# First layer of a recurrent network: a second add of the query products on POOL, key squares on ACT, and a later preparation

## The chip, the cores and the metric

The kernel runs on one core of a Trainium2 chip. The metric is the time of the whole program on the device in microseconds (us), as the median of several runs. The engines named below are PE (the matrix engine), DVE (VectorE), ACT (ScalarE), POOL (GpSimd) and SP, which issues transfers. They run side by side and are held together by counting semaphores.

## What is computed

The network has four layers; each takes a layer norm of `x`, computes a recurrent part `s` and a gate `g`, and sets `x = x + s * g`. The change touches the first layer alone, whose recurrent part is a gated delta rule with 16 heads of size 8 over 256 steps of 32 sequences:

```python
q = (x @ Wq + bq); k = (x @ Wk + bk); v = (x @ Wv + bv)      # each reshaped to heads of D = 8
k = k / (norm(k, axis=-1) + 1e-06)
beta = sigmoid(x @ Wbeta + bbeta)
def step(S, q_t, k_t, v_t, beta_t):
    Sk = einsum('bhde,bhe->bhd', S, k_t)
    S = S + beta_t * einsum('bhd,bhe->bhde', v_t - Sk, k_t)
    return S, einsum('bhde,bhe->bhd', S, q_t)                # output of the step
```

Its output goes through `Wo`, and is gated by the silu of a feed forward part (relu, square, two ternary weight matrices).

## The kernel before

`delta_ffn` runs the first layer. The tokens are cut into NT = 16 tiles of 512 tokens, which are 16 time steps of 32 sequences; one tile is worked off as 8 pairs of steps (PAIRS = 8). The state of the recurrence goes from pair to pair, so the pairs form one long chain of 128, all of it on DVE (`pair`, L569 to L597: two instructions each of the lines L576, L581, L584, L587, L594 and L597). The other engines prepare the next tile and finish the last one beside this chain. Each engine's order is written out by hand in its own block; the engines wait for each other only by semaphores, and an engine never passes a waiting instruction.

What one tile i needs, and what is done for tile i + 1 while the pairs of tile i run:

- ACT evacuates the projections of tile i + 2 from PSUM (`evacuate`, L393, four per tile, the fourth with a sigmoid, which needs a table load) once DVE has turned the tile before (semaphore `turned`). Then comes the square root of the key norms (`root`, L398, with a table load of its own), then the feed forward work.
- DVE turns the four projections of tile i + 1 to token-major form (`turn`, L543), sums the squares of the keys (`norms`, L547), adds 1e-6 and inverts after ACT's root (`inverse`, L551 and L553), and sums the overlap of the two keys of a pair (`overlaps`, L557).
- POOL squares the keys (`squares`, L454), multiplies values by beta (`values`, L460), scales the keys (`keys`, L466 and L470) and multiplies them with each other (L473, what `overlaps` sums), and corrects for the second step of a pair (`correct`, L482 and L485). DVE begins a tile when `prepared` and `lifted` (an ACT copy of the corrected keys to PSUM, L422) are there.
- The outputs: after each pair POOL multiplies the state with the queries (`queries`, L493, 512 products per partition). After every second pair POOL adds the upper half of each group of eight products to the lower half (`halve`, L499), and DVE sums the remaining four (`outputs`, L561). The last quarter of a tile's outputs is summed in the next tile, followed by the turn back (`turn_out`, L568). PE projects it, and POOL gates it (`gate`, L504 and L507, after the multiplication of pair 6 of the next tile).

The names in profile rows carry the prefix `d_`: `d_sq_q` holds the products with the queries, `d_tm` the turned projections, `d_nrm` the norms, `d_sqk` the squared keys.

Of the kernel before, what the change touches and what calls it, by code (L numbers as in the profile page):

```python
# [7 lines left out]
ALU = mybir.AluOpType  # L8
ACT = mybir.ActivationFunctionType
AX = mybir.AxisListType.X  # L10

P = 128
# [3 lines left out]
NT = N // TILE  # L16
# [4 lines left out]
@contextmanager  # L21
def phase(nc, names, inside=None):

    stage = nc.next_id()
    sems = [nc.alloc_semaphore(f"{n}_{stage}") for n in names.split()]
    if inside is not None:
        block, held = inside
        held.extend(sems)
        yield (block, *sems)
        return  # L30
    with nc.Block() as block:
        yield (block, *sems)
    nc.clear_and_free_semaphores(sems)
    nc.all_engine_barrier()  # L34
# [222 lines left out]
H0, D0 = 16, 8  # L257
# [5 lines left out]
def delta_ffn(nc, w, wfc_t, wproj_t, xn, x_in, x_out, x_slots):  # L263
# [7 lines left out]
    with ExitStack() as ctx:  # L271
        def sb(name, shape):
            return ctx.enter_context(nc.sbuf_tensor("d_" + name, shape, F32))
# [8 lines left out]
        tm = sb("tm", [P, 2, 4, TILE])  # L282
        sqk = sb("sqk", [P, STEPS * HL, D0])
# [9 lines left out]
        sq_q = sb("sq_q", [P, STEPS, HL * D0, D0])  # L293
        o_tm = sb("o_tm", [P, TILE])
# [6 lines left out]
        zeros = sb("zeros", [P, TILE])  # L301
        (block, projected, evacuated, turned, sqk_ready, norm2, norm1, shifted, rn_ready, parts, m_ready, c_ready, prepared, s_gated,
         stepped, state_ready, sq_ready, o_part, o_turned, o_projected, s_ready, h_ready, relu_ready, r2_ready, y_ready,
         g_ready, mixed, lifted, gated, zeroed, cleared, halved, x_in0, x_in1) = ctx.enter_context(phase(
             nc, "projected evacuated turned sqk_ready norm2 norm1 shifted rn_ready parts m_ready c_ready prepared s_gated "
             "stepped state_ready sq_ready o_part o_turned o_projected s_ready h_ready relu_ready r2_ready y_ready "
             "g_ready mixed lifted gated zeroed cleared halved x_in0 x_in1"))
        x_ready = (x_in0, x_in1)
        rows_out = x_slots.rearrange("(i p r q) c -> i p r (q c)", p=P, r=4, q=4)
        CLEARS = x_slots.shape[0] // (16 * P)  # L310
# [2 lines left out]
        def slot(a, n):  # L313
            return (max(0, a - 3) + n) % 2

        def out_slot(a):
            return a % 2

        def up_slot(a, n):
            return (a + n) % 2  # L320
# [63 lines left out]
        @block.scalar  # L384
        def _(act):

            def evacuate(a):

                if a:
                    act.wait_ge(turned, a)  # L390
                for n, name in enumerate(("bq", "bk", "bv", "bbeta")):
                    act.wait_ge(projected, a * 4 + n + 1)
                    nc.scalar.activation(fm[:, n], ring[:, slot(a, n)], ACT.Identity if n < 3 else ACT.Sigmoid,  # L393
                                         bias=w[name]).then_inc(evacuated, 1)

            def root(a):
                act.wait_ge(norm2, a + 1)
                nc.scalar.activation(nrm[:], nrm[:], ACT.Sqrt).then_inc(norm1, 1)  # L398

            def out(a):  # L400
                act.wait_ge(o_projected, a + 1)
                if a >= 2:
                    act.wait_ge(gated, a - 1)
                nc.scalar.activation(s[:, a % 2], ring[:, out_slot(a)], ACT.Identity, bias=w["bo"]).then_inc(s_ready, 1)

            def ffn(a):
                for m in range(M):
                    n = a * M + m
                    act.wait_ge(h_ready, n + 1)
                    nc.scalar.activation(r[:, m % 2], ring[:, up_slot(a, m)], ACT.Relu).then_inc(relu_ready, 1)  # L410
                    act.wait_ge(relu_ready, n + 1)
                    if a:
                        act.wait_ge(y_ready, n - M + 1)
                    nc.scalar.activation(r2[:, m], r[:, m % 2], ACT.Square).then_inc(r2_ready, 1)
                act.wait_ge(y_ready, (a + 1) * M)
                if a >= 2:
                    act.wait_ge(gated, a - 1)
                nc.scalar.activation(g[:, a % 2], down[:], ACT.Silu).then_inc(g_ready, 1)

            def lift(a):  # L420
                act.wait_ge(prepared, a * 2 + 1)
                nc.scalar.activation(kb_up[:, a % 2], kb[:, a % 2], ACT.Copy).then_inc(lifted, 1)  # L422

            evacuate(0)
            root(0)
            evacuate(1)
            lift(0)
            for i in range(NT):
                if i + 2 < NT:
                    evacuate(i + 2)  # L430
                if i + 1 < NT:
                    root(i + 1)
                if i:
                    out(i - 1)
                ffn(i)
                if i + 1 < NT:
                    lift(i + 1)
            out(NT - 1)

        @block.gpsimd  # L440
        def _(pool):
            G = nc.gpsimd

            def by_step(ap, f):
                return ap.rearrange("p (t h d) -> p t (h d)", h=HL, d=D0)[:, :, f * HH * D0:(f + 1) * HH * D0]
# [2 lines left out]
                b = tm[:, a % 2, 3].rearrange("p (t c) -> p t c", c=HD)[:, :, f * HH:(f + 1) * HH]  # L448
                return b.unsqueeze(3).broadcast_to([P, STEPS, HH, D0])

            def squares(a):
                pool.wait_ge(turned, a + 1)
                kk = tm[:, a % 2, 1].rearrange("p (th d) -> p th d", d=D0)
                G.tensor_tensor(sqk[:], kk, kk, ALU.mult).then_inc(sqk_ready, 1)  # L454

            def values(a):
                if not a:
                    pool.wait_ge(turned, 1)
                for f in range(2):
                    G.tensor_tensor(vb[:, a % 2, :, f], by_step(tm[:, a % 2, 2], f), beta(a, f), ALU.mult).then_inc(parts, 1)  # L460

# [34 lines left out]
            def halve(i, j):  # L496
                pool.wait_ge(sq_ready, i * PAIRS + 2 * j + 2)
                both = sq_q[:, 4 * j:4 * j + 4].rearrange("p t h e -> p (t h) e")
                G.tensor_tensor(both[:, :, 0:D0 // 2], both[:, :, 0:D0 // 2], both[:, :, D0 // 2:], ALU.add).then_inc(halved, 1)  # L499

            def gate(a):
                pool.wait_ge(s_ready, a + 1)
# [6 lines left out]
                                xt[:, a % 2].rearrange("p (t b) -> p t b", b=B), ALU.add).then_inc(gated, 1)  # L509

            G.memset(zeros[:], 0.0).then_inc(zeroed, 1)
            squares(0)
            values(0)
            keys(0)
            correct(0)
            for i in range(NT):
                more = i + 1 < NT
                for p in range(PAIRS):
                    queries(i, p)
                    if p % 2:  # L520
                        halve(i, p // 2)
                    if p == 0 and more:
                        squares(i + 1)
                    if p == 1 and more:
                        values(i + 1)
                    if p == 3 and more:
                        keys(i + 1)
                    if p == 5 and more:
                        correct(i + 1)
                    if p == 6 and i:  # L530
                        gate(i - 1)
# [3 lines left out]
        def _(dve):  # L535
            V = nc.vector

            def turn(a):

                dve.wait_ge(evacuated, a * 4 + 4)  # L540
                if a >= 2:
                    dve.wait_ge(sq_ready, (a - 1) * PAIRS)
                V.transpose(tm[:, a % 2].rearrange("p n c -> p (n c)"), fm[:].rearrange("p n c -> p (n c)")).then_inc(turned, 1)  # L543

            def norms(a):
                dve.wait_ge(sqk_ready, a + 1)
                V.tensor_reduce(nrm[:], sqk[:], AX, ALU.add).then_inc(norm2, 1)  # L547
# [9 lines left out]
                V.tensor_reduce(c[:], cross[:], AX, ALU.add).then_inc(c_ready, 1)  # L557

            def outputs(i, j):
                dve.wait_ge(halved, i * 4 + j + 1)  # L560
                V.tensor_reduce(o_tm[:, j * P:(j + 1) * P], sq_q[:, 4 * j:4 * j + 4].rearrange("p t h e -> p (t h) e")[:, :, 0:D0 // 2],  # L561
                                AX, ALU.add).then_inc(o_part, 1)

            def turn_out(i):
# [39 lines left out]
            for i in range(NT):  # L604
                more = i + 1 < NT
                dve.wait_ge(lifted, i + 1)
                dve.wait_ge(prepared, 2 * i + 2)
                for p in range(PAIRS):
                    pair(i, p)
                    if p == 0 and more:  # L610
                        turn(i + 1)
                    if p == 1 and i:
                        outputs(i - 1, 3)
                        turn_out(i - 1)
                    if p == 1 and more:
                        norms(i + 1)
                    if p == 2 and more:
                        inverse(i + 1)
                    if p in (3, 5, 7):
                        outputs(i, p // 2 - 1)  # L620
                    if p == 5 and more:
                        overlaps(i + 1)
            outputs(NT - 1, 3)
            turn_out(NT - 1)

# [2800 lines left out]
```

## Time and profile before

| what | value |
|---|---|
| median of 3 runs | 4978.35 us (4972.01 to 4992.69) |
| the profiled execution | 4953.71 us, its span 4952.1 us |
| busy in the span: PE, DVE | 3799.2 us (77%), 3628.7 us (73%) |
| busy in the span: POOL, ACT | 2954.5 us (60%), 2514.5 us (51%) |
| first pair of the first layer starts, last state is done | 76.7 us, 569.9 us |
| of this stretch, one tile in steady state | 31.20 us |

A row of the timeline gives the start of an instruction, its length, the engine, the line and what it writes and reads; `x2` is two of them in a row, and the bracket at the end is the time in which the engine was idle before, and who released it. On DVE an instruction starts before the one ahead of it has drained, so the distance between two starts is some hundredths of a microsecond shorter than the duration of the first. This distance is called the slot of an instruction here.

### The profile page before, as it was taken

Reading aid. Unit: us, or ns where it says so; the run is one execution under the profiler, and the core shown is the slowest. Engines: PE = TensorE matmul, PEld = TensorE weight load, DVE = VectorE, ACT = ScalarE, POOL = GpSimd, SP = SyncE. Lnnn points to the kernel's source line nnn. Section 1 sums busy time; section 2 is a strip of 40 time slices with the busy share of each in tenths; the row PEclk is TensorE's granted clock in tenths of the full one; section 3 lists DMA queues with packets and bytes.
Section 4 is the critical chain, followed back from the end, with each engine's and each line's share of the span. In section 5 each row is a group of like instructions: output and inputs, shape, how many; then the busy total and the mean of one; then the engine's idle time right before and its main releaser. Section 6 shows DMA issues by size and latency. Waiting matters only on the chain. (4 is left out here: it accounts for less than half of the span.)

```text
span 4952.1 us, 46565 instructions
## 1 busy us (share of the span) xinstructions
PE 3799.2 (77%) x13159; PEld 1741.4 (35%) x13222; DVE 3628.7 (73%) x5288; ACT 2514.5 (51%) x3881; POOL 2954.5 (60%) x2245
## 2 busy tenths in 40 slices
PE   5444475999649978888887799898979777777776
PEld 2111122764216633333332455453423222222222
DVE  6999774124547669999998644555543899999998
ACT  4444431344437766666664344445355655555554
POOL 3888566017254469999994311114420899889987
PEclk7777788999869999999999899999989999999998
DMA  1110201213211134444441423221200444444343
GB/s 50 43 43 9 84 34 52 68 55 82 94 54 58 43 129 155 156 155 154 155 156 69 97 41 45 41 38 48 64 7 34 144 135 139 136 136 141 128 141 98
DMA packets 161698, 434.77 MB, mean 88 GB/s; under 512 B 28150, under 2 KB 51384, under 8 KB 160048
## 3 DMA queue, kind: packets, MB, share of 16 engines
q1 hardware_dynamic: 142512, 374.41, 25.0%
q0 software_dynamic: 18944, 57.57, 3.4%
q8 instruction: 98, 1.61, 0.1%
q14 instruction: 144, 1.18, 0.1%
HBM read 363.67 MB, written 68.68 MB: 87 GB/s over the span
## 5 line engine op out<-in xcount | busy, mean ns | idle before, releaser
L1659 ACT ACTIVATE mb_h<-m_dt,m_a_neg 128x512 f32<-128x512 f32 x1024 | 665.0, 681 | 724.0 <-DVE r L1814 333.6
L1518 PE MATMUL mb_y<-r,m_diag_y 128*128 128x512 f32 x1024 | 548.5, 671 | 273.2 <-POOL r L1739 164.6
L1805 DVE TENSOR_TENSOR_SCAN mb_h<-mb_h,m_u 128x1024 f32<-128x1024 f32 x320 | 734.0, 2294 | 10.8 <-DVE mb_h L1794 0.5
L1762 POOL TENSOR_TENSOR m_u<-m_bsb,m_xs 128x1024 f32<-128x1024 f32 x256 | 600.1, 2368 | 175.6 <-DMA m_bsb<-bc_rows 175.6
L1762 POOL TENSOR_TENSOR m_u<-m_bsb,m_dtx 128x1024 f32<-128x1024 f32 x256 | 596.1, 2360 | 49.7 <-DVE m_dtx L1846 27.9
L1518 PE MATMUL mb_y<-m_hc,w_common 128*128 128x512 f32 x1024 | 497.0, 625 | 151.8 <-DVE m_hc L1814 85.7
L1805 DVE TENSOR_TENSOR_SCAN m_hs<-mb_h,m_u 128x1024 f32<-128x1024 f32 x192 | 437.6, 2279 | 1.7 <-POOL m_u L1762 1.7
L1518 PEld LDWEIGHTS mb_y<-r,m_diag_y 128*128 128x128 f32 x1024 | 196.2, 207 | 620.0 <-POOL r L1739 244.9
L2288 DVE TENSOR_REDUCE at_mx<-at_ps_s 128x4 f32<-128x512 f32 (+1 forms) x256 | 242.8, 957 | 218.7 <-PE at_ps_s L2102 218.6
L1739 POOL TENSOR_TENSOR r<-m_hs,m_csb 128x1024 f32<-128x1024 f32 x128 | 308.3, 2409 | 117.1 <-DVE m_hs L1805 116.7
L1518 PEld LDWEIGHTS mb_y<-m_hc,w_common 128*128 128x128 f32 x1024 | 191.1, 197 | 450.0 <-issue 192.0
L2220 ACT ACTIVATE at_pt<-at_ps_c 128x512 f32<-128x512 f32 x384 | 229.4, 608 | 160.8 <-DMA r<-y_slots,l_slots 60.8
L2246 POOL CAST at_nm<-at_mx 128x16 bf16<-128x16 f32 x64 | 12.6, 196 | 500.1 <-DVE at_mx L2288 500.1
L1791 DVE SCALAR_TENSOR_TENSOR m_u<-mb_h,m_u 128x1024 f32<-128x1024 f32 x256 | 307.8, 1202 | 0.0
L343 PE MATMUL d_ring<-r,w_l 128*128 128x512 f32 x128 | 91.2, 856 | 224.1 <-ACT d_fm L393 222.2
L1477 PE MATMUL mb_w<-r,m_wconv 128*128 128x512 f32 x512 | 233.2, 609 | 14.1 <-PEq L34 7.0
L1814 DVE TENSOR_TENSOR m_hc<-mb_h,m_csb 128x1024 f32<-128x1024 f32 x192 | 235.1, 1224 | 3.6
L493 POOL TENSOR_TENSOR d_sq_q<-d_state,d_tm 128x512 f32<-128x512 f32 x128 | 161.7, 1269 | 91.2 <-DVE d_state L597 91.1
L1009 POOL DMA_INDIRECT x_slots<-r,l_slots x128 | 142.9, 1117 | 86.8 <-DVEq L1053 45.3
L2127 PE MATMUL at_ps_c<-at_q,at_k 75*128 75x512 bf16 x384 | 154.1, 402 | 43.5 <-ACT at_pt L2220 27.7
L1739 POOL TENSOR_TENSOR m_hc<-m_hs,m_csb 128x1024 f32<-128x1024 f32 x64 | 150.8, 2356 | 32.4 <-DVE m_hs L1805 32.4
L2102 PE MATMUL at_ps_s<-at_k,at_q 72*128 72x256 bf16 (+1 forms) x1024 | 169.6, 260 | 0.0
(516 smaller groups left out, 8475.4 us busy)
## 6 DMA issues: line engine op xcount, KB each, us to landing
m_bsb<-bc_rows SPq DMA_DIRECT2D x256, 512.0 KB, 4.9
m_csb<-bc_rows SPq DMA_DIRECT2D x256, 512.0 KB, 4.0
at_q<-q_parts SPq DMA_DIRECT2D x144, 128.0 KB
x_slots<-d_zeros SPq DMA_DIRECT2D x8, 1024.0 KB, 5.1
kept_x<-r SPq DMA_DIRECT2D x2, 4096.0 KB, 14.1
xg_xg<-x_slots SPq DMA_DIRECT2D x32, 256.0 KB, 2.7
y_slots<-xg_yo POOLq DMA_DIRECT2D x32, 256.0 KB, 2.3
xl_xg<-x_slots SPq DMA_DIRECT2D x32, 256.0 KB, 2.7
```

The lines of the kernel that those rows point to most:

```text
L493: G.tensor_tensor(sq_q[:, 2 * p:2 * p + 2], state[:, n % 3], qt.unsqueeze(2).broadcast_to([P, 2 * HL, D0, D0]), ALU.mult).then_inc(sq_read ...
L1477: mm = nc.tensor.matmul(ps_w[:, h], wconv[:, k, h * P:(h + 1) * P], padded_tile(hp, k)(a), start=k == 0, stop=k == TAPS - 1)
L1518: mm = nc.tensor.matmul(ps_y[:, h], weight, hc[:, q % RING, s], start=False, stop=g == GROUPS - 1 and s == SG - 1)
L1659: ins = nc.scalar.activation(ps_h[:, q % 2, s], dt[:, i % 2, h], ACT.Exp, scale=a_neg[:, n:n + 1])
L1739: nc.gpsimd.tensor_tensor(hc[:, q % RING], hs[:, k % 2], csb[:, n % RING], ALU.mult).then_inc(hp_ready, 1)
L1762: nc.gpsimd.tensor_tensor(u[:, q % RING], bsb[:, n % RING], dtx[:, i % 2, h].unsqueeze(1).broadcast_to([P, SG, TILE]), ALU.mult).then_inc( ...
L1791: V.scalar_tensor_tensor(out=flat(u[:, q % RING]), in0=flat(ps_h[:, q % 2]), scalar=-1.0, in1=flat(u[:, q % RING]), op0=ALU.add, op1=ALU.m ...
L1805: V.tensor_tensor_scan(flat(to), flat(ps_h[:, q % 2]), flat(u[:, q % RING]), 0.0, ALU.mult, ALU.add).then_inc(h_ready, 1)
L1814: V.tensor_tensor(hc[:, q % RING], ps_h[:, q % 2], csb[:, n % RING], ALU.mult).then_inc(hc_ready, 1)
L2102: mm = nc.tensor.matmul(ps_s[:, g % 2, d, 0:keys], q9[0:PARTS, slot, g * QPK + d, col:col + P], k9[0:PARTS, slot, g, row:row + keys], star ...
L2220: nc.scalar.activation(pt[:, u % 8], ps_c[:, u % 2], ACT.Exp).then_inc(exp_ready, 1)
L2288: V.tensor_reduce(mx[:, n % 2, g * QPK:(g + 1) * QPK], ps_s[:, g % 2, :, 0:(n % 2 + 1) * P], AX, ALU.max, negate=True).then_inc(max_ready, 1)
```

## The change

Three things are edited, all in `delta_ffn`.

- `halve` on POOL gets a second add: it waits for its own first add, then adds the products 2 and 3 of each group to 0 and 1 (new semaphore `summed`). `outputs` on DVE waits for `summed` and sums two values per output instead of four.
- The squares of the keys move from POOL to ACT (`squares`, new on ACT). ACT runs them for tile i + 1 ahead of `evacuate(i + 2)`.
- The preparation of tile i + 1 comes one pair later on DVE: `turn` after pair 1 instead of pair 0 (behind the last outputs and the turn back of the tile before), `norms` after pair 2 instead of 1, `inverse` after pair 3 instead of 2. On POOL `values` comes at pair 2 instead of 1, `keys` at pair 4 instead of 3. `correct` on POOL and `overlaps` on DVE stay at pair 5.

```diff
+            def squares(a):
+                act.wait_ge(turned, a + 1)
+                nc.scalar.activation(sqk[:].rearrange("p th d -> p (th d)"), tm[:, a % 2, 1], ACT.Square).then_inc(sqk_ready, 1)
...
             evacuate(0)
+            squares(0)
             root(0)
             evacuate(1)
             lift(0)
             for i in range(NT):
+                if i + 1 < NT:
+                    squares(i + 1)
                 if i + 2 < NT:
                     evacuate(i + 2)
...
                 G.tensor_tensor(both[:, :, 0:D0 // 2], both[:, :, 0:D0 // 2], both[:, :, D0 // 2:], ALU.add).then_inc(halved, 1)
+                pool.wait_ge(halved, i * 4 + j + 1)
+                G.tensor_tensor(both[:, :, 0:2], both[:, :, 0:2], both[:, :, 2:4], ALU.add).then_inc(summed, 1)
...
-                    if p == 0 and more:
-                        squares(i + 1)
-                    if p == 1 and more:
+                    if p == 2 and more:
                         values(i + 1)
-                    if p == 3 and more:
+                    if p == 4 and more:
                         keys(i + 1)
                     if p == 5 and more:
                         correct(i + 1)
...
             def outputs(i, j):
-                dve.wait_ge(halved, i * 4 + j + 1)
-                V.tensor_reduce(o_tm[:, j * P:(j + 1) * P], sq_q[:, 4 * j:4 * j + 4].rearrange("p t h e -> p (t h) e")[:, :, 0:D0 // 2],
+                dve.wait_ge(summed, i * 4 + j + 1)
+                V.tensor_reduce(o_tm[:, j * P:(j + 1) * P], sq_q[:, 4 * j:4 * j + 4].rearrange("p t h e -> p (t h) e")[:, :, 0:2],
                                 AX, ALU.add).then_inc(o_part, 1)
...
                     pair(i, p)
-                    if p == 0 and more:
-                        turn(i + 1)
                     if p == 1 and i:
                         outputs(i - 1, 3)
                         turn_out(i - 1)
                     if p == 1 and more:
+                        turn(i + 1)
+                    if p == 2 and more:
                         norms(i + 1)
-                    if p == 2 and more:
+                    if p == 3 and more:
                         inverse(i + 1)
                     if p in (3, 5, 7):
                         outputs(i, p // 2 - 1)
                     if p == 5 and more:
                         overlaps(i + 1)
```

On DVE, in the middle of the first layer, this stands from the turn of the next tile (L543) to the sum of its squared keys (L547) before:

```order
L543 STREAM_TRANSPOSE d_tm<-d_fm 128x2048
L576 TENSOR_TENSOR d_prod<-d_state,d_kb_up 128x256 x2
L581 TENSOR_REDUCE d_small<-d_prod 128x32 x2
L584 TENSOR_TENSOR d_small<-d_vb,d_small 128x32 x2
L587 TENSOR_TENSOR d_outer<-d_small,d_k 128x256 x2
L594 TENSOR_TENSOR d_state<-d_state,d_outer 128x128 x2
L597 TENSOR_TENSOR d_state<-d_state,d_outer 128x128 x2
L561 TENSOR_REDUCE d_o_tm<-d_sq_q 128x128
L568 STREAM_TRANSPOSE d_o_fm<-d_o_tm 128x512
L547 TENSOR_REDUCE d_nrm<-d_sqk 128x64
```

and now, with the outputs of the tile before ahead of it:

```order
L561 TENSOR_REDUCE d_o_tm<-d_sq_q 128x128
L568 STREAM_TRANSPOSE d_o_fm<-d_o_tm 128x512
L543 STREAM_TRANSPOSE d_tm<-d_fm 128x2048
L576 TENSOR_TENSOR d_prod<-d_state,d_kb_up 128x256 x2
L581 TENSOR_REDUCE d_small<-d_prod 128x32 x2
L584 TENSOR_TENSOR d_small<-d_vb,d_small 128x32 x2
L587 TENSOR_TENSOR d_outer<-d_small,d_k 128x256 x2
L594 TENSOR_TENSOR d_state<-d_state,d_outer 128x128 x2
L597 TENSOR_TENSOR d_state<-d_state,d_outer 128x128 x2
L547 TENSOR_REDUCE d_nrm<-d_sqk 128x64
```

The last quarter of the outputs and the turn back have moved ahead of the turn, so that fewer instructions lie between the turn and what follows from it.

On ACT, at the same place, this stands from the copy of the corrected keys to the root of the norms before:

```order
L422 ACTIVATE d_kb_up<-d_kb 128x512
L393 ACTIVATE d_fm<-d_ring,w_l_63 128x512 x3
L393 ACT_TABLE_LOAD
L393 ACTIVATE d_fm<-d_ring,w_l_63 128x512
L398 ACT_TABLE_LOAD
L398 ACTIVATE d_nrm<-d_nrm 128x64
```

and now (the numbers of lines behind the new function have moved by 4):

```order
L426 ACTIVATE d_kb_up<-d_kb 128x512
L398 ACTIVATE d_sqk<-d_tm 128x512
L393 ACTIVATE d_fm<-d_ring,w_l_63 128x512 x3
L393 ACT_TABLE_LOAD
L393 ACTIVATE d_fm<-d_ring,w_l_63 128x512
L402 ACT_TABLE_LOAD
L402 ACTIVATE d_nrm<-d_nrm 128x64
```

The square stands ahead of the four evacuations and the root, and brings no table load of its own.

On POOL, this stands around the scaling of the keys (L466 to L473), from the products of pairs 2 and 3 on, before:

```order
L493 TENSOR_TENSOR d_sq_q<-d_state,d_tm 128x512 x2
L499 TENSOR_TENSOR d_sq_q<-d_sq_q 128x128x4
L466 TENSOR_TENSOR d_k<-d_tm,d_nrm 128x8x32 x2
L470 TENSOR_TENSOR d_kb<-d_k,d_tm 128x8x32 x2
L473 TENSOR_TENSOR d_cross<-d_k,d_kb 128x256
```

and now, from the products of pair 3 on:

```order
L494 TENSOR_TENSOR d_sq_q<-d_state,d_tm 128x512
L500 TENSOR_TENSOR d_sq_q<-d_sq_q 128x128x4
L502 TENSOR_TENSOR d_sq_q<-d_sq_q 128x128x2
L494 TENSOR_TENSOR d_sq_q<-d_state,d_tm 128x512
L467 TENSOR_TENSOR d_k<-d_tm,d_nrm 128x8x32 x2
L471 TENSOR_TENSOR d_kb<-d_k,d_tm 128x8x32 x2
L474 TENSOR_TENSOR d_cross<-d_k,d_kb 128x256
```

The keys now stand behind the products of pair 4, which wait for the state of that pair, and a second add stands behind each first one.

## Rows read from the trace of the kernel before

**Rows 1.** One steady tile: window; busy PE, PEld, DVE, ACT, POOL; clock; DMA share; GB/s

```profile
297.05:328.25 31.20, 13.97 (x26) 5.31 (x26) 30.85 (x106) 13.20 (x19) 25.39 (x27) 0.72 0.12 42
```

**Rows 2.** Timeline of DVE in this tile

```profile
297.05 2.31 DVE L543 STREAM_TRANSPOSE d_tm<-d_fm 128x2048 f32<-128x2048 f32 x1 [0.26 <-POOL d_sq_q L493]
299.28 0.71 DVE L576 TENSOR_TENSOR d_prod<-d_state,d_kb_up 128x256 f32<-128x256 f32 x2
...
303.60 0.64 DVE L547 TENSOR_REDUCE d_nrm<-d_sqk 128x64 f32<-128x512 f32 x1
304.16 0.74 DVE L576 TENSOR_TENSOR d_prod<-d_state,d_kb_up 128x256 f32<-128x256 f32 x2
...
307.15 0.19 DVE L551 TENSOR_SCALAR d_nrm<-d_nrm 128x64 f32<-128x64 f32 x1
...
307.85 0.69 DVE L576 TENSOR_TENSOR d_prod<-d_state,d_kb_up 128x256 f32<-128x256 f32 x2
...
317.38 0.68 DVE L561 TENSOR_REDUCE d_o_tm<-d_sq_q 128x128 f32<-128x512 f32 x1
317.97 0.41 DVE L557 TENSOR_REDUCE d_c<-d_cross 128x32 f32<-128x256 f32 x1
318.30 0.74 DVE L576 TENSOR_TENSOR d_prod<-d_state,d_kb_up 128x256 f32<-128x256 f32 x2
```

**Rows 3.** Lines of DVE and POOL in the first layer (count | busy us, mean ns | idle before)

```profile
L561 DVE TENSOR_REDUCE d_o_tm<-d_sq_q 128x128 f32<-128x512 f32 x64 | 43.3, 677 | 2.9 <-POOL d_sq_q L499 2.9
L543 DVE STREAM_TRANSPOSE d_tm<-d_fm 128x2048 f32<-128x2048 f32 x15 | 34.7, 2310 | 3.9 <-POOL d_sq_q L493 3.9
L454 POOL TENSOR_TENSOR d_sqk<-d_tm 128x512 f32<-128x512 f32 x16 | 16.6, 1039 | 12.3 <-DVE d_tm L543 12.3
```

**Rows 4.** Timeline of ACT in this tile, from the end of the turn on

```profile
299.39 1.26 ACT L393 ACTIVATE d_fm<-d_ring,w_l 128x512 f32<-128x512 f32 x2 [7.51 <-DVE d_tm L543]
...
304.95 1.28 ACT L398 ACT_TABLE_LOAD   x1
306.25 0.26 ACT L398 ACTIVATE d_nrm<-d_nrm 128x64 f32<-128x64 f32 x1
...
308.92 0.63 ACT L414 ACTIVATE d_r<-d_r 128x512 f32<-128x512 f32 x1
309.46 0.58 ACT L410 ACTIVATE d_r<-d_ring 128x512 f32<-128x512 f32 x1
```

**Rows 5.** Timeline of all engines in tile 0, from which two engines stand

```profile
79.69 2.30 DVE L543 STREAM_TRANSPOSE d_tm<-d_fm 128x2048 f32<-128x2048 f32 x1
...
88.36 0.26 ACT L398 ACTIVATE d_nrm<-d_nrm 128x64 f32<-128x64 f32 x1
...
88.65 0.26 DVE L551 TENSOR_SCALAR d_nrm<-d_nrm 128x64 f32<-128x64 f32 x1
...
89.42 0.69 DVE L576 TENSOR_TENSOR d_prod<-d_state,d_kb_up 128x256 f32<-128x256 f32 x2
```

**Rows 6.** Timeline of POOL in the steady tile

```profile
307.31 1.28 POOL L493 TENSOR_TENSOR d_sq_q<-d_state,d_tm 128x512 f32<-128x512 f32 x1 [1.08 <-DVE d_state L597]
310.95 1.28 POOL L493 TENSOR_TENSOR d_sq_q<-d_state,d_tm 128x512 f32<-128x512 f32 x1 [2.35 <-DVE d_state L597]
312.31 1.27 POOL L499 TENSOR_TENSOR d_sq_q<-d_sq_q 128x512 f32<-128x512 f32 x1
313.54 1.25 POOL L466 TENSOR_TENSOR d_k<-d_tm,d_nrm 128x256 f32<-128x256 f32 x2
...
316.06 0.73 POOL L473 TENSOR_TENSOR d_cross<-d_k,d_kb 128x256 f32<-128x256 f32 x1
...
320.54 0.63 POOL L482 TENSOR_TENSOR d_corr<-d_kb,d_c 128x256 f32<-128x256 f32 x1
...
323.09 1.26 POOL L493 TENSOR_TENSOR d_sq_q<-d_state,d_tm 128x512 f32<-128x512 f32 x1
...
326.88 1.26 POOL L493 TENSOR_TENSOR d_sq_q<-d_state,d_tm 128x512 f32<-128x512 f32 x1
```

More of the change, by code:

```diff
@@ L303, in delta_ffn @@
          stepped, state_ready, sq_ready, o_part, o_turned, o_projected, s_ready, h_ready, relu_ready, r2_ready, y_ready,
-         g_ready, mixed, lifted, gated, zeroed, cleared, halved, x_in0, x_in1) = ctx.enter_context(phase(
+         g_ready, mixed, lifted, gated, zeroed, cleared, halved, summed, x_in0, x_in1) = ctx.enter_context(phase(
              nc, "projected evacuated turned sqk_ready norm2 norm1 shifted rn_ready parts m_ready c_ready prepared s_gated "
              "stepped state_ready sq_ready o_part o_turned o_projected s_ready h_ready relu_ready r2_ready y_ready "
-             "g_ready mixed lifted gated zeroed cleared halved x_in0 x_in1"))
+             "g_ready mixed lifted gated zeroed cleared halved summed x_in0 x_in1"))
         x_ready = (x_in0, x_in1)
@@ L449, in beta, with values @@
                 return b.unsqueeze(3).broadcast_to([P, STEPS, HH, D0])
-            def squares(a):
+            def values(a):
                 pool.wait_ge(turned, a + 1)
[L453 to L458, printed above, removed]
                 for f in range(2):
@@ L511, in _ @@
             G.memset(zeros[:], 0.0).then_inc(zeroed, 1)
-            squares(0)
             values(0)
```

## The prediction, written before the changed kernel had run

> **What bounds the kernel now.** I read the busy time by engine first, then, since the change touches the first layer alone, one steady tile of it, and then the timelines of DVE, ACT and POOL in that tile. In the 31.20 us of a tile DVE is busy for 30.85 us, POOL for 25.39 us and ACT for 13.20 us [rows 1]. DVE's order is fixed, and its only wait is one ahead of the turn, for POOL's last product: 3.9 us in all, in 13 tiles [rows 3]. So DVE sets the pace here; whatever takes time off its slots shortens the layer, and every wait put into its row lengthens it. POOL and ACT have room in busy time, but DVE also waits for single results of theirs, and when these come is the question.
>
> **What DVE saves.** Summing 512 products into 128 outputs takes 677 ns [rows 3] and a slot of 0.59 us (317.38 to 317.97) [rows 2]. The new form reads 256. The nearest row is the reduction of 256 into 32, 0.41 us with a slot of 0.33 us [rows 2]; that of 512 into 64 takes 0.64 us against 0.68 us for 512 into 128 [rows 2], so the greater number of outputs adds some 0.03 us. I take a slot of 0.36 us, with ends 0.33 and 0.40. That is 64 x 0.23 = **14.7 us** less (12.2 to 16.6). The wait ahead of the turn goes too: the turn now stands behind pair 1, long after the last product of the tile before. With the overlap of neighbours that a wait breaks, it costs some 0.36 us per tile, 13 x 0.36 = **4.7 us** less. Together -19.4 us.
>
> **The wait at `inverse`.** This comes from the order on DVE and ACT. Before, ACT begins at 299.39, as soon as the turn is over (297.05 + 2.31 = 299.36), and its four evacuations, two table loads and the root end at 306.25 + 0.26 = 306.51 [rows 2, 4]. So the root is there 7.15 us behind the end of the turn. DVE comes for it at 307.15, 7.79 us behind the turn: 0.64 us of slack. Now both change for the worse. On ACT the square stands ahead of the evacuations; a square of this size has a slot of 0.54 us (308.92 to 309.46) [rows 4], I take 0.57, which makes the root 7.72 us late, 7.75 us with the handover of 0.03 (88.36 + 0.26 = 88.62 to 88.65) [rows 5]. The evacuation of the values waits for a product on PE that itself waits for the first evacuation, so the whole chain shifts. On DVE, outputs and turn back no longer lie in between: the way is turn (slot 299.28 - 297.05 = 2.23), pair 2 (2.97), `norms` (304.16 - 303.60 = 0.56), pair 3 (307.15 - 304.16 = 2.99) [rows 2], 8.75 us from the start of the turn, 6.44 us from its end. DVE waits 7.75 - 6.44 = **1.31 us**. That such a wait exists is shown by tile 0 of the kernel before, which has no outputs in between: there L551 starts at 88.65, 0.03 us behind the end of the root [rows 5]. A woken DVE also needs 0.77 us for the two instructions (88.65 to 89.42) instead of 0.70 [rows 2, 5], so 1.38 us. Tiles 1 to 13 have it, 13 x 1.38 = 17.9 us; tile 0 has no table load for the sigmoid, its root comes 6.63 us (88.62 - 81.99) behind the turn [rows 5] and would come at 7.23: some 0.6 us more than before. Tile 14 evacuates nothing. Sum **+18.5 us**.
>
> **The wait at `overlaps`.** `keys` moved behind pair 4, `overlaps` stayed behind pair 5. Call D the moment at which DVE has issued pair 4. POOL takes up the product 0.16 us later (307.15 to 307.31) [rows 2, 6]. Its slot is 1.23, the keys take 316.06 - 313.54 = 2.52, and the cross product 0.73 [rows 6]; with a handover of 0.05 the overlap can start at D + 0.16 + 1.23 + 2.52 + 0.73 + 0.05 = D + 4.69. DVE comes to it after pair 5 (3.00) and one sum of outputs (0.36), at D + 3.36. It waits **1.33 us**. Before, the keys stood behind pair 3 and had a whole pair more. 15 tiles, **+19.9 us**. I see nothing that covers this: POOL is idle ahead of pair 4's product, so it cannot be earlier than the state.
>
> **The second add on POOL.** 64 adds of 128 x 256. The rows of that size take 0.64 us (L466, two in 1.25) to 0.73 us (L473) [rows 6]; both operands are whole here as in L473, so 0.73, slot 0.69. Each also waits for the first add: a dependent start costs 1.36 instead of 1.23 (310.95 to 312.31) [rows 6], 0.13 more. Per tile 4 x 0.82 = 3.3 us, less one square of 1.04 us [rows 3]: POOL goes from 25.4 to some 27.6 us, under DVE's. Its order matters in one place, the last quarter. From D: product 5 at 4.59, first add 5.95, second 7.31, `correct` 8.00 (2.55 long, 320.54 to 323.09), product 6 at 10.55, gate and all until product 7 at 14.34 (3.79 later, 323.09 to 326.88), first add 15.70, second 17.06 to 17.79 [rows 6]. DVE, from D: overlap 4.69, two pairs 11.02, outputs 11.38, two pairs of the next tile 17.35, and then it wants the last quarter. That was covered before, since it had no second add; now it waits some 0.45 us. With 0.64 us per add it would be 0.25. I take 0.4, in the 14 tiles that have a gate before them: **+5.6 us**. The keys for the next tile are ready at 10.55, DVE wants them at 11.38, and ACT's copy fits in between, so the tile's start is covered. At the very end one more add and one shorter sum stand in line: +0.6 us.
>
> A rule of the Trainium skill bears on this price alone. "GPSIMD Engine Reference", section 3.1, gives 4497 ns for an fp32 add of 2048 elements, so by elements one of 256 would take about 0.6 us as an estimate, and the last-quarter wait would be 0.25 us: a sum lower by 2 us. The row L473, the same kind with two whole operands, has 0.73 us; I go by it.
>
> **The square on ACT** costs nothing by itself: ACT has 18 us of room in a tile, and the order of the built kernel shows no table load with it. Its price is the 0.57 us in the chain above. The turn comes 3.4 us later in the tile, ACT's feed forward with it, but it ends some 16 us behind the turn, and the next thing due from ACT, the copy of the keys, only after 21 us.
>
> **The sum.** -14.7 - 4.7 + 18.5 + 19.9 + 5.6 + 0.6 = **+25.2 us**. A steady tile goes from 31.20 us to about 33.0. On the profiled execution that is 4953.7 + 25 = 4979 us; the median of the runs is 24.6 us above that execution, and the same step on it gives **5003 us**, +0.5%.
>
> **Rivals.**
> - One of the two large waits is smaller than walked. For `inverse`: ACT would have to finish within 6.44 us of the turn, against 7.15 before without the square; against it speaks tile 0. For `overlaps`: the keys and product would need 3.15 us instead of 4.48. If one of them failed, the step would be 25 - 18 = +6 us, 4985 us.
> - The other side: neither wait decides, because DVE comes to both places later than I walk it, and the saved slots are all that shows. The deciding points are the same 6.44 us and D + 3.36. It would give -14.7 - 4.7 + 0.6 = -19 us, 4959 us, faster, but by 0.4%. For it speaks only that DVE has no such waits in the steady tile now.
> - POOL takes over the pace: the narrow add, in pieces of two elements, costs as much as the wide one, 1.27 us instead of 0.73 [rows 6]. Each tile then has 4 x 0.54 more, POOL at 29.8 us, and the last-quarter wait holds two of these adds, 1.1 us more: 15 x 1.1 = 16 us, 5020 us. Against it: the halving in pieces of four costs the same as the products, 1.27 and 1.28 us [rows 6].
>
> **How the numbers follow.** Forecast 0.74 (0.39 of it above +0.5%, which is 24.9 us, 0.35 below, since the sum lies on this edge with an uncertainty of some 6 us from the slots and as much from the medians); one wait only 0.09; neither 0.04; POOL's pace 0.09; other costs on DVE 0.04. A measurement of this kernel can tell about 0.5% from no change. Slower by over 0.5%: 0.39 + 0.09 + 0.03 = 0.51; within 0.5%: 0.45; faster: 0.04, since even the best case gives less than 0.5%. The sum with all slots at their good ends is +20, at their bad ends +30; with the medians' own 8 us and half of the POOL case the range is 4984 to 5020.
>
> **What the profile will show.** A tile of about 33.0 us instead of 31.2; L561 near 0.43 us; idle time before L551 of about 1.3 us in 13 tiles, released by ACT's root; idle before L557 of about 1.3 us in 15, released by POOL's cross product; idle before L561 of 0.3 to 0.5 us in 14; none before L543. The forecast is wrong if a steady tile takes under 32 us or over 34, or if an operation on POOL with two-element pieces takes over 0.8 us.

## The result, and the profile after

| | before | changed |
|---|---|---|
| median of 20 runs each, on one chip | 4979.8 us | 4996.57 us |
| range of the runs | 4965.26 to 5002.14 | 4982.65 to 5016.52 |
| span of the profiled execution | 4952.1 us | 4982.8 us |
| one steady tile of the first layer | 31.20 us | 32.63 us |
| first pair's start to the start of the last sum of outputs | 496.7 us | 516.7 us |

The ratio is 1.0034, with a 95% interval of 1.0023 to 1.0045: the changed kernel is 17 us slower. The forecast was 5003 us, +25. The last row of the table, called the stretch from here on, holds all that the change touches, and has grown by 20.0 us. The two profiled spans differ by 30.7 us; the 10.7 us outside the stretch lie in layers that are the same in both, and are the difference of two single executions. So tiles and stretch are compared below, with the ratios of the runs and their intervals beside them. Steady tiles repeat to a few hundredths of a microsecond; one early tile of the kernel before takes 31.55 us.

Busy times in one steady tile of the changed kernel (window, busy PE, PEld, DVE, ACT, POOL, the clock, DMA):

```profile
310.78:343.41 32.63, 13.97 (x26) 5.43 (x26) 30.02 (x107) 13.72 (x20) 26.82 (x30) 0.71 0.11 40
```

Against [rows 1] DVE is busy for 0.8 us less in a tile that is 1.4 us longer: 2.6 us of waiting where there were 0.35. The timeline of DVE shows where; the bracket is the idle time ahead of an instruction and its releaser:

```profile
309.69 0.42 DVE L561 TENSOR_REDUCE d_o_tm<-d_sq_q 128x128 f32<-128x256 f32 x1
310.14 0.71 DVE L568 STREAM_TRANSPOSE d_o_fm<-d_o_tm 128x512 f32<-128x512 f32 x1
310.78 2.27 DVE L543 STREAM_TRANSPOSE d_tm<-d_fm 128x2048 f32<-128x2048 f32 x1
...
319.13 0.47 DVE L597 TENSOR_TENSOR d_state<-d_state,d_outer 128x128 f32<-128x128 f32 x2
320.74 0.26 DVE L551 TENSOR_SCALAR d_nrm<-d_nrm 128x64 f32<-128x64 f32 x1 [1.13 <-ACT d_nrm L402]
321.03 0.55 DVE L553 RECIPROCAL d_nrm<-d_nrm 128x64 f32<-128x64 f32 x1
321.50 0.36 DVE L561 TENSOR_REDUCE d_o_tm<-d_sq_q 128x128 f32<-128x256 f32 x1
321.78 0.73 DVE L576 TENSOR_TENSOR d_prod<-d_state,d_kb_up 128x256 f32<-128x256 f32 x2
...
327.77 0.41 DVE L561 TENSOR_REDUCE d_o_tm<-d_sq_q 128x128 f32<-128x256 f32 x1
329.46 0.42 DVE L557 TENSOR_REDUCE d_c<-d_cross 128x32 f32<-128x256 f32 x1 [1.28 <-POOL d_cross L474]
```

The turn (L543) no longer has a wait in front of it, as against [rows 2]; the two waits that the prediction names stand ahead of L551 and L557. The lines of the first layer, with the busy time, the mean in ns, and the idle time ahead of them in all tiles, to be held against [rows 3]:

```profile
L561 DVE TENSOR_REDUCE d_o_tm<-d_sq_q 128x128 f32<-128x256 f32 x64 | 25.6, 400 | 5.6 <-POOL d_sq_q L502 3.9
L557 DVE TENSOR_REDUCE d_c<-d_cross 128x32 f32<-128x256 f32 x16 | 6.7, 420 | 22.4 <-POOL d_cross L474 22.4
L551 DVE TENSOR_SCALAR d_nrm<-d_nrm 128x64 f32<-128x64 f32 x16 | 4.3, 269 | 16.4 <-ACT d_nrm L402 16.4
...
L502 POOL TENSOR_TENSOR d_sq_q<-d_sq_q 128x256 f32<-128x256 f32 x64 | 39.2, 612 | 5.0
```

And ACT between the turn and the root, to be held against [rows 4]:

```profile
313.08 0.63 ACT L398 ACTIVATE d_sqk<-d_tm 128x512 f32<-128x512 f32 x1 [10.53 <-DVE d_tm L543]
313.62 1.25 ACT L393 ACTIVATE d_fm<-d_ring,w_l 128x512 f32<-128x512 f32 x2
316.45 0.69 ACT L393 ACTIVATE d_fm<-d_ring,w_l 128x512 f32<-128x512 f32 x1 [1.59 <-PE d_ring L343]
...
319.16 1.28 ACT L402 ACT_TABLE_LOAD   x1
320.45 0.26 ACT L402 ACTIVATE d_nrm<-d_nrm 128x64 f32<-128x64 f32 x1
```

The turn ends at 310.78 + 2.27 = 313.05, the root at 320.45 + 0.26 = 320.71, 7.66 us later. The square has a slot of 0.54 us, the wait for PE's product of the values has kept its 1.59 us behind it, and so the chain has moved as a whole.

### The profile page after: what moved, and what is told of

The parts are those of the page before. It is cut to its first block and busy times, and to the rows that moved or that the text cites. A ratio compares the mean times of both kernels' runs of the same rounds, so it can differ in the third digit from the quotient of the medians.

```text
span 4982.8 us, 46692 instructions
## 1 busy us (share of the span) xinstructions
PE 3808.9 (76%) x13222; PEld 1742.8 (35%) x13222; DVE 3617.3 (73%) x5288; ACT 2522.7 (51%) x3897; POOL 2978.8 (60%) x2293
```

## The experiments

Two questions were open. The first is whether the parts of the change cost what the sum gives them. The second is what a wait costs. In theory B of the texts on record each wait is a cost of its own, as the sum and the first rival treat it. In theory A POOL's chain of work sets the tile, and a wait of DVE inside it costs nothing by itself. The results first:

| kernel | tile, expected | tile | stretch | ratio to before (95%) |
|---|---|---|---|---|
| before | | 31.20 | 496.7 | |
| changed | 33.0 | 32.63 | 516.7 | 1.0034 (1.0023 to 1.0045) |
| e1, overlaps behind pair 6 | A 32.63, B 31.3 | 32.62 | 516.0 | 1.0031 (1.0018 to 1.0044) |
| e3, the same, gate late | A 31.6, B 31.2 | 31.62 | 501.3 | 1.0001 (0.9988 to 1.0014) |
| e4, root early | 31.35 | 31.38 | 499.3 | 0.9999 (0.9985 to 1.0014) |
| e8, keys at pair 3 | 31.07 | 31.19 | 496.1 | 0.9993 (0.9976 to 1.001) |
| e5, second add alone | A 32.3, B below 31.2 | 32.30 | 511.2 | 1.0028 (1.0014 to 1.0041) |
| e6, square on ACT alone | 31.2 | 31.20 | 498.0 | 1.0001 (0.999 to 1.0013) |
| e7, late preparation alone | 32.75 | 33.24 | 526.0 | 1.0063 (1.0043 to 1.0082) |
| e10, e7 with L551 into PSUM | 32.65 | 32.70 | 518.1 | 1.0029 (1.0017 to 1.0041) |
| e9, three moves on the changed | 29.8 | 29.79 | 475.0 | 0.9958 (0.9943 to 0.9973) |
| e11, e9 without the second add | 30.83 | 30.85 | 490.8 | 0.9979 (0.9961 to 0.9996) |

The first four experiments ran on a chip on which every kernel takes some 290 us longer, the one before too (5269.08 us), in later layers; the tiles of the first layer are not affected. Each ratio is to runs of the kernel before on the same chip. e7 has four executions, the others six to ten; one of e3's ten, of 13194 us, is not in its ratio.

### Is a wait of DVE a cost of its own?

e1 changes one line of the changed kernel:

```diff
-                    if p == 5 and more:
+                    if p == 6 and more:
                         overlaps(i + 1)
```

> The changed kernel, with the sum of the overlaps on DVE behind pair 6 instead of pair 5; POOL is untouched. In the changed kernel DVE waits 1.3 us per tile ahead of L557. Theory A (POOL's chain sets the tile): from product 4 to the second add of the last quarter POOL works without a gap for 17.3 us, and DVE waits at its end anyway, 0.2 us. Then the wait only moves: none ahead of L557, about 0.5 us for the corrected values ahead of the next tile, about 1.0 us ahead of the first L561 of a tile. A tile stays at 32.63 us, the stretch from the first pair to the last sum of outputs stays within 3 us of 516.7 us. Theory B (each wait is a cost of its own): the tile falls by 1.35 us to 31.3 us, the stretch to about 496 us, the kernel is 20 us faster than the changed one, equal to the kernel before.

Measured: a tile of 32.62 us. 1.3 us of waiting per tile are gone ahead of L557, and nothing has been gained. DVE's timeline in a tile of e1:

```profile
330.04 0.41 DVE L557 TENSOR_REDUCE d_c<-d_cross 128x32 f32<-128x256 f32 x1
...
333.37 0.41 DVE L561 TENSOR_REDUCE d_o_tm<-d_sq_q 128x128 f32<-128x256 f32 x1
334.26 0.75 DVE L576 TENSOR_TENSOR d_prod<-d_state,d_kb_up 128x256 f32<-128x256 f32 x2 [0.48 <-ACT d_kb_up L426]
...
341.25 0.42 DVE L561 TENSOR_REDUCE d_o_tm<-d_sq_q 128x128 f32<-128x256 f32 x1 [0.91 <-POOL d_sq_q L502]
```

L557 now runs without a wait, and the same time turns up ahead of the next tile's first pair (0.48) and ahead of the first sum of outputs (0.91). The releaser of the first is ACT's copy of the corrected keys, which follows POOL. Theory A holds: from the product of pair 4 to the second add of the last quarter POOL works without a gap, and DVE cannot end its tile before that. In the changed kernel this is the stretch from 292.32 to 309.65, with no idle time in brackets between the two rows:

```profile
292.32 1.27 POOL L494 TENSOR_TENSOR d_sq_q<-d_state,d_tm 128x512 f32<-128x512 f32 x1 [1.94 <-DVE d_state L597]
...
309.04 0.61 POOL L502 TENSOR_TENSOR d_sq_q<-d_sq_q 128x256 f32<-128x256 f32 x1
...
319.69 1.26 POOL L494 TENSOR_TENSOR d_sq_q<-d_state,d_tm 128x512 f32<-128x512 f32 x1 [1.12 <-DVE d_state L597]
```

(The third row is wanted further down.) The other half of the loop, from there over the turn, ACT's root and pair 4, belongs to DVE and ACT.

e3 adds to e1 that POOL's gate of the tile before comes behind the last quarter:

```diff
-                    if p == 6 and i:
+                    if p == 7 and i:
                         gate(i - 1)
```

> As the run with the later overlaps, and POOL's gate of the tile before behind the last quarter's adds (pair 7) instead of ahead of product 7. Theory A: this takes 2.57 us out of POOL's chain where DVE waits for it, so the gain of the later overlaps shows at last, except for 0.5 us of waiting for the corrected values: tile 32.63 - 1.36 - 0.20 + 0.54 = 31.6 us, stretch about 502 us, some 5 us slower than the kernel before. Theory B: the gate is not DVE's business, 31.1 to 31.3 us with or without it.

Measured: 31.62 us and 501.3 us. The gate's 2.57 us were no business of DVE's, but stood in the chain it waits for; only with them out of the way do the later overlaps pay. What is left is the half microsecond for the corrected keys. The gate's move without the later overlaps was not run.

e8 leaves DVE alone and puts POOL's keys back:

```diff
-                    if p == 4 and more:
+                    if p == 3 and more:
                         keys(i + 1)
```

> The changed kernel, with the scaling of the keys on POOL back at pair 3 (behind the two adds) instead of pair 4. This uses POOL's idle time ahead of product 4 (1.94 us) and shortens its chain. Theory A and B: no wait ahead of L557, none ahead of the first L561; the wait ahead of L551 stays. Tile 32.63 - 1.36 - 0.20 = 31.07 us, stretch about 493 us, 3 to 5 us faster than the kernel before. Against the run with the later overlaps this tells whether it is the place of POOL's work or DVE's wait that counts.

Measured: 31.19 us, where 31.07 was expected: 1.44 us of 1.56. A wait of 0.13 us has stayed ahead of the first sum of outputs (its instruction starts at 330.58, 0.13 us behind its slot), which I had said would go. The one line is worth all that the change lost. In the changed kernel POOL is idle for 1.9 us ahead of the product of pair 4, and the keys stand behind this gap. DVE has issued pair 5 by 295.16, and POOL takes up its product only at 296.76, 1.60 us later. In e8 the keys fill the gap, and the product of pair 5 starts at 317.63, 0.16 us after DVE has issued the pair (317.47). The difference is the 1.44 us that the tile gains.

### The wait for the root

In e4, ACT takes the root ahead of the fourth evacuation:

```diff
                 if i + 2 < NT:
-                    evacuate(i + 2)
+                    evacuate(i + 2, range(3))
                 if i + 1 < NT:
                     root(i + 1)
+                if i + 2 < NT:
+                    evacuate(i + 2, (3,))
```

> The changed kernel, with ACT's root of the norms ahead of the fourth evacuation (sigmoid) instead of behind it; the square stays first. Both theories say that the wait ahead of L551 comes from what ACT does between the turn and the root (7.66 us); without the fourth evacuation and its table load the root is there 5.7 us behind the turn, DVE comes after 6.5 us. No wait ahead of L551, tile 32.63 - 1.28 = 31.35 us, stretch 499 us, about 18 us faster than the changed kernel and 2 us slower than the one before. If a wait of over 0.3 us stays ahead of L551, the chain is not the one told.

Measured: 31.38 us and 499.3 us, and no idle time ahead of L551 (L555 in this kernel) in any tile but the one prepared before the loop. This wait was a cost of its own, 1.25 us per tile. It lies in the other half of the loop, which POOL's chain only enters with pair 4.

### The parts of the change, one at a time

e5 is the kernel before with the new add and the shorter sum:

```diff
+                pool.wait_ge(halved, i * 4 + j + 1)
+                G.tensor_tensor(both[:, :, 0:2], both[:, :, 0:2], both[:, :, 2:4], ALU.add).then_inc(summed, 1)
...
-                dve.wait_ge(halved, i * 4 + j + 1)
-                V.tensor_reduce(o_tm[:, j * P:(j + 1) * P], sq_q[:, 4 * j:4 * j + 4].rearrange("p t h e -> p (t h) e")[:, :, 0:D0 // 2],
+                dve.wait_ge(summed, i * 4 + j + 1)
+                V.tensor_reduce(o_tm[:, j * P:(j + 1) * P], sq_q[:, 4 * j:4 * j + 4].rearrange("p t h e -> p (t h) e")[:, :, 0:2],
```

> The kernel before with the second add on POOL and the shorter sum on DVE alone; squares on POOL, preparation at its old pairs. DVE saves 64 x 0.26 = 16.6 us of slots. Theory A (POOL's chain): in the kernel before POOL works without a gap from product 3 to product 7, and the turn of the next tile waits for product 7; two adds of 0.70 us come into that chain, and what DVE saves in between is waited away. Tile 18.86 + 13.48 = 32.3 us against 31.20, stretch about 513 us against 496.7, 16 us slower than before. Theory B (DVE is full, POOL has room): the stretch falls to about 480 us, 17 us faster.

Measured: 32.30 us and 511.2 us. The row of its timeline that takes back what DVE saves:

```profile
335.41 2.31 DVE L545 STREAM_TRANSPOSE d_tm<-d_fm 128x2048 f32<-128x2048 f32 x1 [1.94 <-POOL d_sq_q L493]
```

The idle time ahead of the turn has gone from 0.26 us [rows 2] to 1.94 us. A second wait, of 0.33 us, has come ahead of each tile's first pair, for the corrected keys. With DVE 99% and POOL 81% busy in a tile of the kernel before, moving work from DVE to POOL loses 14.5 us, because the turn waited for the end of POOL's chain, not for POOL's average.

e6 is the kernel before with the squares on ACT:

```diff
+            def squares(a):
+                act.wait_ge(turned, a + 1)
+                nc.scalar.activation(sqk[:].rearrange("p th d -> p (th d)"), tm[:, a % 2, 1], ACT.Square).then_inc(sqk_ready, 1)
...
+                if i + 1 < NT:
+                    squares(i + 1)
                 if i + 2 < NT:
                     evacuate(i + 2)
```

> The kernel before with the squares of the keys on ACT alone. The root comes 0.54 us later, 7.69 us behind the turn, and DVE wants it after 7.79: covered by 0.1 us. POOL loses 1.04 us where it is idle later anyway. Tile 31.2 us, stretch 496.7 within 2 us (tile 0 has 0.5 more), no difference in the time. Rival: the square on ACT costs 0.5 us per tile, 8 us.

Measured: 31.20 us and 498.0 us. The 0.54 us on ACT are covered by the 0.64 us of slack ahead of `inverse`, except in tile 0. It costs something only where that slack is gone.

e7 is the kernel before with the later preparation:

```diff
-                    if p == 0 and more:
+                    if p == 1 and more:
                         squares(i + 1)
-                    if p == 1 and more:
+                    if p == 2 and more:
                         values(i + 1)
-                    if p == 3 and more:
+                    if p == 4 and more:
                         keys(i + 1)
```

and the moves of `turn`, `norms` and `inverse` on DVE as in the change.

> The kernel before with the preparation one pair later alone (squares on POOL behind the first half add, no second add). The wait ahead of the turn goes (-0.36 us per tile); ahead of L551 some 0.8 us appear (root 7.18 us behind the turn, DVE there after 6.44, and 0.07 for a woken DVE), ahead of L557 some 1.1 us. No wait ahead of L561. Tile 31.20 - 0.36 + 0.81 + 1.10 = 32.75 us, stretch about 518 us, 20 us slower than before: the later preparation alone costs as much as the whole change. Rival: it costs nothing by itself, and the whole change's loss comes from the second add.

Measured: 33.24 us and 526.0 us, 29 us more than before, where I had expected 21. The waits ahead of L551 (0.61 us) and L557 (1.0 us) are near the ones expected, but L551 itself does not take 0.19 us as in [rows 2]:

```profile
326.32 0.79 DVE L551 TENSOR_SCALAR d_nrm<-d_nrm 128x64 f32<-128x64 f32 x1 [0.61 <-ACT d_nrm L398]
327.14 0.55 DVE L553 RECIPROCAL d_nrm<-d_nrm 128x64 f32<-128x64 f32 x1
```

and this is what POOL runs beside it:

```profile
325.79 1.26 POOL L493 TENSOR_TENSOR d_sq_q<-d_state,d_tm 128x512 f32<-128x512 f32 x1 [1.12 <-DVE d_state L597]
327.13 1.27 POOL L499 TENSOR_TENSOR d_sq_q<-d_sq_q 128x512 f32<-128x512 f32 x1
```

L551 ends at 327.11, 0.06 us behind POOL's product (327.05). In the changed kernel it ends at 321.00, and POOL's product of pair 3, the third row shown with e1, at 319.69 + 1.26 = 320.95. There only 0.21 us of the product were left when L551 started.

e10 tests this: L551 writes to PSUM instead of SBUF.

```diff
-                V.tensor_scalar_add(nrm[:], nrm[:], 1e-6).then_inc(shifted, 1)
+                V.tensor_scalar_add(shift_ps, nrm[:], 1e-6).then_inc(shifted, 1)
                 dve.wait_ge(shifted, a + 1)
-                V.reciprocal(nrm[:], nrm[:]).then_inc(rn_ready, 1)
+                V.reciprocal(nrm[:], shift_ps).then_inc(rn_ready, 1)
```

> The kernel with the later preparation alone, but L551 (adds 1e-6 to the norms) writes its 128x64 result to PSUM, and the reciprocal reads it from there. In that kernel L551 takes 0.79 us in a steady tile instead of 0.19, and ends 0.06 us behind the end of POOL's product of pair 3 that runs beside it. Theory: an instruction of this form (one operand and one result in SBUF) is held by POOL's running instruction; with the result in PSUM it is not: L551 near 0.2 us, the wait ahead of it stays near 0.6 us, tile 33.24 - 0.6 = 32.65 us, stretch 526 - 8 = 518 us. Rival: DVE is slow because it was woken by ACT, whatever the operand: L551 stays at 0.79 us, tile 33.24 us.

Measured, in DVE's timeline, with POOL's product of pair 3 running from 318.76 to 320.02:

```profile
319.30 0.23 DVE L552 TENSOR_SCALAR d_small<-d_nrm 128x64 f32<-128x64 f32 x1 [0.61 <-ACT d_nrm L399]
319.56 0.56 DVE L554 RECIPROCAL d_nrm<-d_small 128x64 f32<-128x64 f32 x1
```

The instruction (L552 here) takes 0.23 us although DVE was woken by ACT after the same 0.61 us; the tile is 32.70 us, the stretch 518.1 us. So the 0.79 us was not the waking, but the SBUF operand beside a running POOL instruction. The trace of the changed kernel says the same from the other side. Before the first pair, DVE is woken by ACT while POOL runs nothing, and L551 takes 0.20 us:

```profile
69.28 0.20 DVE L551 TENSOR_SCALAR d_nrm<-d_nrm 128x64 f32<-128x64 f32 x1 [0.88 <-ACT d_nrm L402]
```

The ratio of e10's runs, 1.0029, stands for some 14 us, less than the 21 us of its stretch, which lies just above the interval's upper end of 20 us. The stretch is taken from one execution; why the two differ is not known.

The three parts alone cost 14.5, 1.3 and 29.3 us of stretch, 45 us together, and the whole change costs 20.0 us. Two losses of the parts are absent from the whole: there the turn does not stand behind POOL's last product (no idle time ahead of L543), and L551 takes 0.26 us in steady tiles instead of 0.79 us. One loss is new: the square, which cost nothing in e6, lengthens the idle time ahead of L551 from 0.61 us in e7 to 1.13 us.

### A version without the waits

e9 is the changed kernel with e4's root, e8's keys and e3's gate; the overlaps stay behind pair 5.

> The changed kernel with three moves: ACT's root ahead of the sigmoid evacuation, the keys on POOL back at pair 3, the gate on POOL behind the last quarter's adds. Every wait of DVE named so far should be gone: tile 32.63 - 1.28 - 1.36 - 0.20 = 29.8 us, which is the sum of DVE's slots; stretch about 478 us, 38 us less than the changed kernel and 18 to 20 us less than the one before. Time about 4960 us against 4980. If a wait stays on DVE, it is named by its line.

Measured: 4958.51 us against 4980.43 us for the kernel before on the same chip, ratio 0.9958 (0.9943 to 0.9973), 22 us faster by the medians and 21.7 us by the stretch. A tile of it:

```profile
292.37:322.15 29.78, 14.89 (x26) 5.91 (x26) 29.71 (x107) 13.84 (x20) 26.78 (x30) 0.73 0.12 45
```

DVE is busy for 29.71 of 29.78 us. The three moves together give 2.84 us per tile, which is the sum of the three waits named (1.28 + 1.36 + 0.20). e4 and e8 alone gave 1.25 and 1.44 us of it.

e11 takes the second add out of e9 again, as in e5 but the other way round.

> The kernel with all three moves, with the second add on POOL taken out again and DVE summing four values. If DVE alone sets the pace there, the second add is worth exactly its slots on DVE, 4 x 0.26 = 1.04 us per tile: tile 29.79 + 1.04 = 30.83 us, stretch 475.0 + 16.6 = 491.6 us, some 5 us faster than the kernel before. Rival: POOL's extra adds cost something there too, then the tile is below 30.8 us.

Measured: 30.85 us and 490.8 us. Once the order is right, the second add is worth 1.06 us per tile, 15.8 us of the stretch, the same add that loses 14.5 us in e5. By the ratios it is worth some 10 us (0.9979 against 0.9958), and the two intervals overlap; the tiles decide here.

## Why the prediction was right, and where it was not

The sign, the mechanisms of the large waits and the range held: 4996.57 us is in 4984 to 5020, and the step of 17 us is 8 us smaller than forecast. The signs that the prediction asked for were there too: a tile of 32.63 us, L561 at 400 ns, idle time of 1.13 us ahead of L551 and 1.27 us ahead of L557, and none ahead of L543. Ahead of L561 there was 0.12 us where 0.3 to 0.5 was forecast. Term by term, with the slots of all tiles in the traces of the kernel before and of the changed one:

| step of the sum | forecast | measured |
|---|---|---|
| shorter sums on DVE (63 in the stretch; slot 0.33 for 0.59) | -14.7 | -17.4, of which a longer slot of the product behind gives back 0.7: -16.7 |
| no wait ahead of the turn | -4.7 | -4.9, and -0.6 for the turn's own slot, 2.19 for 2.23 |
| wait at `inverse` (DVE is free at 319.53, starts at 320.74) | +18.5 | 13 x 1.28 + 1.0 = +17.7 |
| wait at `overlaps` | +19.9 | 15 x 1.35 = +20.2 |
| wait for the last quarter (309.49 to 309.69 = 0.20) | +5.6 | 14 x 0.20 = +2.8 |
| the end (idle ahead of the last sum 3.87 for 2.91) | +0.6 | +1.0 |
| slots of `norms` (0.60 for 0.56) and `overlaps` (0.34 for 0.33) | 0 | +0.6 |
| sum | +25.2 | +20.1 |

This is the growth of the stretch, 20.0 us. The 17 us of the medians have an interval of some 11 to 22 us, which holds it.

- **"The wait at `inverse`"** held: 1.21 us instead of 1.31. The square's slot was 0.54 instead of 0.57, and the turn took 2.27 instead of 2.31 us and had a slot of 2.19. The 0.07 us for "a woken DVE" was right in size and wrong in its cause: a woken L551 takes 0.20 us where POOL is idle (the row shown with e10), and 0.26 us here, where it ends 0.05 us behind POOL's running product. Tile 0, from which the 0.07 was read, is the same case: L551 ends at 88.91, and an instruction of POOL's ends at 88.86. In tile 0 of the changed kernel more of POOL's product was left, L551 took 0.55 us, and the tile lost 1.0 us instead of 0.6.
- **"The wait at `overlaps`"** held to 0.02 us, and POOL's idle time ahead of pair 4's product was there (1.94 us).
- **"The second add on POOL"** was mis-sized: 0.612 us instead of 0.73, just outside the two rows that I had as ends (0.64 and 0.73), and POOL is busy for 26.8 us of a tile instead of 27.6. With 0.61 in the same walk the wait for the last quarter comes out at 0.2 us, as measured. The estimate from the figure of the Trainium skill, "GPSIMD Engine Reference", section 3.1, was about 0.6 us, and the trace agrees with it. I had gone by L473 because it has two whole operands as the new add; why L473 needs 0.73 us and L502 0.61 us for as many elements, no run here tells.
- **"What DVE saves"**: the slot was 0.33 us, the good end; the greater number of outputs cost nothing. This term was mis-sized by 2.0 us.
- **The first rival's price was wrong in kind.** It took the wait at `overlaps` away and subtracted 18 us. e1 took it away, and the time stayed. The walk from D to the last quarter, in the same prediction, shows why: POOL is late by 0.45 us for the last quarter even with DVE waiting 1.33 us in between, so DVE's wait lay beside POOL's chain. The sum came out right because the last-quarter wait was computed behind the other; as separate prices the terms mislead.
- The other side (neither wait decides) and POOL's pace by a dear narrow add did not come about; but by e1, e3 and e5 POOL's order, not its price, did set part of the pace, at 82% busy.

The sum stood on the edge of the 0.5% that I took as what a measurement can tell from no change, and I gave 0.51 to slower by more and 0.45 to within. The result, 0.34%, is within; with 20 executions of each kernel its interval (0.23% to 0.45%) is nevertheless clear of zero. The two mis-sized terms, the last quarter's wait behind the second add (2.8 us) and DVE's sums (2.0 us), make up nearly all of the 5 us between the forecast and the stretch.

## What to carry to other kernels

An engine that is 80% busy has room only where its idle time lies: the same adds on POOL, four of 0.61 us per tile, lost 14.5 us in one order of instructions and gained 15.8 us in another. Before a wait is priced, follow the chain of its releaser to the next place where the waiting engine needs it; if the releaser runs on without a gap to that place, removing the wait moves it. And when a step is moved later, look at both ends: what its producer must still do (ACT's square and table loads), and what cover on the waiting engine was moved away with it.

## What the runs showed of the hardware

L551 on DVE, a TENSOR_SCALAR of 128 x 64 in fp32 with operand and result in SBUF, takes 0.19 us where no instruction of POOL's is running as it starts. Where more than that is left of a running one, L551 ends 0.05 to 0.06 us behind the end of that one: 0.26 us with 0.21 us left and 0.55 us with 0.50 us left in the changed kernel, 0.79 us with 0.73 us left in the steady tiles of e7, and 1.08 us with 1.03 us left in e7's tile 0, as the summary of the buffer `d_nrm` in e7 shows (count: least/median/greatest in ns, first and last start):

```profile
L551 DVE TENSOR_SCALAR d_nrm<-d_nrm x16: 187/785/1084, 70.8 to 558.2; 128x64 f32<-128x64 f32 x16
L553 DVE RECIPROCAL d_nrm<-d_nrm x16: 552/553/553, 71.1 to 558.5; 128x64 f32<-128x64 f32 x16
```

With the result in PSUM it takes 219 to 229 ns in all 16 tiles of e10. The reciprocal, of the same size and from SBUF to SBUF too, is not held beside POOL's instructions (552 to 553 ns in e7); why it is not, no run here tells. The Trainium skill, "GPSIMD Engine Reference", section 8, says that POOL shares its SBUF interfaces with VectorE, with contention for DVE instructions in a 2-port mode or with two SBUF inputs; "VectorE: DVE Perf Modes", section "Mode 2×_2P — use both read ports for one tensor", counts fp32 `tensor_scalar` between SBUF tensors among the 2-port ones and excludes PSUM operands. The traces agree with both for L551, and the size here is the rest of POOL's running instruction.
